# Four heads' scores in one run over four PSUM banks, with the transpositions in the dense products' banks

## What is computed

```python
qkv = x @ c_attn_w + c_attn_b                       # q, k, v
k = concat([img @ uk_w.T + uk_b, k_word], axis=1)   # one image key in front
v = concat([img @ uv_w.T + uv_b, v_word], axis=1)
scores = einsum('bhqd,bhkd->bhqk', q, k) / sqrt(32) # causal: kj <= qi + 1
attn = softmax(scores + mask)
x = x + (einsum('bhqk,bhkd->bhqd', attn, v) @ c_proj_w + c_proj_b)
xw = x @ Wx + b
h_t = tanh(h_{t-1} @ Wh + xw_t)                     # 512 steps, one after the other
return x + h
```

## Time and profile before

| | |
|---|---|
| median of 3 runs | 1696.64 us (1696.03 to 1708.65) |
| the profiled execution | 1703.19 us, its span 1701.4 us |
| mean granted TensorE clock | 0.981 |
| TensorE busy | 1613.0 us (95%), 32749 matmul instructions |
| VectorE busy | 792.6 us (47%) |
| ScalarE busy | 661.7 us (39%) |
| GpSimd busy | 185.6 us (11%) |
| moved by DMA | 130.24 MB, mean 77 GB/s |

### The profile page before, as it was taken

One profiled execution on the slowest core, in us unless ns is written; L12 is line 12 of the kernel. 1 busy time (PEld: TensorE's weight loads), 2 busy tenths in 40 slices (PEclk: granted clock), 3 DMA queues, 4 the chain that ended last, 5 costly groups with the idle time before them and its releaser, 6 DMA issues.

```text
span 1701.4 us, 74131 instructions
## 1 busy us (share of the span) xinstructions
PE 1613.0 (95%) x32749; PEld 1254.3 (74%) x32749; DVE 792.6 (47%) x2687; ACT 661.7 (39%) x2257; POOL 185.6 (11%) x300
## 2 busy tenths in 40 slices
PE   7889999999999999999999999999999999999775
PEld 6667777777777878777777877777777777777554
DVE  3444444454445454454545555454554554554221
ACT  3434333433334443443444444444434444443111
POOL 2111111111011010111011010110101111000000
PEclk9869999999999999999999999999999999999999
DMA  6322111222223122332323323233332443321000
GB/s 232 87 50 70 42 54 52 69 65 61 56 59 92 57 83 67 85 83 69 83 62 110 103 83 90 65 115 97 91 86 72 124 111 99 93 71 34 15 9 15
DMA packets 167903, 130.24 MB, mean 77 GB/s; under 512 B 54264, under 2 KB 153112, under 8 KB 167072
## 3 DMA queue, kind: packets, MB, share of 16 engines
q1 hardware_dynamic: 153792, 92.92, 19.3%
q0 software_dynamic: 13792, 32.58, 6.8%
HBM read 100.00 MB, written 25.43 MB: 74 GB/s over the span
## 4 chain that ended last, share of the span: by engine, by line
PE 88%; issue 3%; ACT 3%; DVE 2%; DMA 2%; SPq 1%; POOL 0%; DVEq 0%; ACTq 0%; POOLq 0%
PE rec L1047 26%; PE turned L977 11%; PE scores L966 9%; PE dense L495 8%; PE dense L496 7%; PE dense L497 7%; PE rec L1038 6%; PE pv L994 5%; PE pv L1012 2%; PE scores L1047 2%; DVE pre L873 1%; ACT states L727 1%; PE dense L948 1%; PE dense L1054 1%; DMA xin<-x 1%
## 5 line engine op out<-in xcount | busy, mean ns | idle before, releaser
L1047 PE MATMUL rec<-wh,states 128*32 128x128 f32 x15360 | 516.9, 275 | 28.8 <-ACT states L727 27.4
L1047 PEld LDWEIGHTS rec<-wh,states 128*32 128x32 f32 x15360 | 400.1, 110 | 125.3 <-ACT states L727 67.9
L679 ACT ACTIVATE probs<-probs,nmax 128x64 f32<-128x64 f32 (+7 forms) x512 | 270.6, 529 | 250.0 <-DVE nmax L818 247.5
L873 DVE STREAM_TRANSPOSE pre<-rec 128x128 f32<-128x128 f32 x480 | 151.8, 316 | 450.6 <-PE rec L1047 449.0
L727 ACT ACTIVATE states<-pre 128x32 f32<-128x32 f32 x512 | 133.0, 260 | 450.8 <-DVE pre L873 448.9
L818 DVE CUSTOM_DVE_ANT_0 probs<-scores,msk,nimg 128x64 f32<-128x64 f32 (+7 forms) x512 | 245.6, 514 | 38.8 <-PE scores L966 31.6
L977 PE MATMUL turned<-ident,probs 128*128 128x128 f32 (+1 forms) x1280 | 242.4, 291 | 8.7 <-ACT probsT L686 8.0
L977 PEld LDWEIGHTS turned<-ident,probs 128*128 128x128 f32 (+1 forms) x1280 | 132.4, 135 | 82.9 <-issue 68.6
L966 PE MATMUL scores<-kt,q 32*64 32x64 f32 (+7 forms) x2048 | 186.1, 431 | 0.3 <-DVE nmax L818 0.2
L827 DVE COPY probsT<-turned 128x128 f32<-128x128 f32 (+3 forms) x256 | 124.9, 488 | 77.1 <-PE turned L977 71.7
L495 PE MATMUL dense<-xT_hi,wqkv_hi 128*128 128x256 f32 x488 | 150.9, 309 | 1.4 <-DVE xT_lo L775 1.4
(11 more groups left out here) (148 smaller groups left out, 1779.9 us busy)
## 6 DMA issues: line engine op xcount, KB each, us to landing
vbuf<-v_dram SPq DMA_DIRECT2D x64, 192.0 KB, 2.8
xin<-x SPq DMA_DIRECT2D x64, 128.0 KB, 3.0
v_dram<-vbuf POOLq DMA_DIRECT2D x64, 128.0 KB, 2.7
out<-outs POOLq DMA_DIRECT2D x32, 256.0 KB, 4.2
vbuf<-v_dram SPq DMA_DIRECT2D x64, 128.0 KB, 2.4
kt<-k_dram SPq DMA_DIRECT2D x16, 512.0 KB, 4.1
vbuf<-v_dram SPq DMA_DIRECT2D x32, 256.0 KB, 3.3
k_dram<-knew POOLq DMA_DIRECT2D x60, 128.0 KB, 2.6
```

What stands on the lines that cost most here:

```text
L679: act.activation(probs[:, g % PROBS, 0:n], probs[:, g % PROBS, 0:n], ACT.Exp, scale=-1.0, bias=nmax[:, e, h:h + 1], accum_out=rowsum[:, e, ...
L873: dve.transpose(pre_all, rec_bank(g // GROUP)[:, 0:P]).then_inc(pre_ready, 1)
L1047: last = pe.matmul(rec_bank(g // GROUP)[Q * j:Q * j + Q, 0:P], state_tile(g - 1)[:, f, :], wh[:, f, P * j:P * j + P], start=False, stop=f ...
```

## The change

- The banks: `scores` has four banks, `turned` is gone, and the transpositions become jobs of the dense banks, in the same turn as the dense products. The semaphores `turned_copied` go with it; a copy of a transposition signals `dense_copied` of its bank.
- The scores of four units are issued together, at every fourth slot, in place of two at every second. The scores of unit g wait for the minimum of unit g − 4. No recurrence step is laid inside a run.
- The minimum and the exponential become an event of their own (`softmax`): its place in the four slots of a run is written by:

```diff
-            if u % 2 == 0:
-                emit([("score", v, 0, 0.07 + 0.107 * keys(g) / P) for v in (u, u + 1)])
+            if u % HC == 0:
+                emit([("score", v, 0, 0.06 + 0.06 * keys(g) / P) for v in range(u, u + HC)])
+            emit([("softmax", v, 0, 0.0) for v in ((u,), (u, u + 1), (u + 1,), ())[u % HC]])
...
             share -= side[0][3]
             emit([side.pop(0)])
+            if out[-1][0] == "vfirst":
+                share -= side[0][3]
+                emit([side.pop(0)])
...
-                if main[at][0] == "score" and main[at][1] % 2 == 0:
+                if main[at][0] == "score" and main[at][1] % HC < HC - 1:
                     continue
...
-        if kind in DENSE_KINDS and kind != "v":
+        if kind in DENSE_KINDS + ("turn",) and kind != "v":
             count = 2 if ("xsteps", 0, 0) in JOB else 3
...
-        scores = [ctx.enter_context(nc.psum_tensor(f"scores{i}", [P, BANK], F32)) for i in range(2)]
-        turned = [ctx.enter_context(nc.psum_tensor(f"turned{i}", [P, BANK], F32)) for i in range(2)]
+        scores = [ctx.enter_context(nc.psum_tensor(f"scores{i}", [P, BANK], F32)) for i in range(HC)]
...
+        def turns_copied(group):
+            return dict((JOB["turn", g, 0][0], JOB["turn", g, 0][1] + 1) for g in range(HC * group, HC * group + HC))
...
                 elif kind == "turn" and g % 2:
-                    act.copy(probsT[:, g % TURNED, 0:n], turned[1][:, 0:n]).then_inc(turned_copied[1], 1)
+                    act.copy(probsT[rows, g % TURNED, 0:n], bank(kind, g, 0)[rows, 0:n]).then_inc(copied(kind, g, 0), 1)
...
                 elif kind == "turn" and g % 2 == 0:
-                    dve.tensor_copy(probsT[:, g % TURNED, 0:n], turned[0][:, 0:n]).then_inc(turned_copied[0], 1)
+                    dve.tensor_copy(probsT[rows, g % TURNED, 0:n], bank(kind, g, 0)[rows, 0:n]).then_inc(copied(kind, g, 0), 1)
...
-                    if g > 1:
-                        pe.wait_ge(shifted_ready, g - 1)
+                    if g == 0:
+                        pe.wait_ge(image_ready, 1)
+                    if g >= HC:
+                        pe.wait_ge(shifted_ready, g - HC + 1)
...
-                        last = pe.matmul(scores[g % 2][W * b:W * b + W, 0:n], q[rows, trip % 2, c, at:at + W],
+                        last = pe.matmul(scores[g % HC][W * b:W * b + W, 0:n], q[rows, trip % 2, c, at:at + W],
                                          heads_tile(group)[rows, b, :], start=True, stop=True, skip_group_check=True)
...
                 elif kind == "turn":
-                    if g > 1:
-                        pe.wait_ge(turned_copied[g % 2], g // 2)
+                    wait_bank(pe, kind, g, 0)
...
                 elif kind == "pv":
-                    for parity in range(2):
-                        pe.wait_ge(turned_copied[parity], 2 * g + 2)
+                    for held, count in turns_copied(g).items():
+                        pe.wait_ge(dense_copied[held], count)
```

More of the change, by code:

```diff
@@ L60 @@
 LAGS = {
-    "DVE": {"xsplit": 0.7, "k": 0.2, "v": 0.2, "imgscore": 0.2, "score": 0.2, "turn": 0.2, "imgprob": 0.0,
+    "DVE": {"xsplit": 0.7, "k": 0.2, "v": 0.2, "imgscore": 0.2, "softmax": 0.2, "turn": 0.2, "imgprob": 0.0,
             "total": 0.5, "norm": 0.2, "attnlow": 0.9, "proj": 0.2, "step": 0.1, "hist": 0.8,
             "vimg": 0.2, "wproj": 0.8},
-    "ACT": {"xsplit": 0.0, "q": 0.2, "score": 0.8, "turn": 0.2, "imgprob": 0.2, "imgturn": 0.2,
+    "ACT": {"xsplit": 0.0, "q": 0.2, "softmax": 0.8, "turn": 0.2, "imgprob": 0.2, "imgturn": 0.2,
             "rowturn": 0.2, "norm": 0.6, "step": 0.5, "out": 0.2, "wproj": 0.0},
@@ L417, in attention_recurrence @@
         turned_ready = sem("turned_ready")
-        turned_copied = [sem(f"turned_copied{i}") for i in range(2)]
         pv_done = sem("pv_done")
@@ L652, in _ @@
                 high_qkv(i)
-            for f, d in enumerate(scores + turned):
+            for f, d in enumerate(scores):
                 act.wait_ge(setup_turned, C + 2 + f)
@@ L673, in _ @@
                                    bias=bqk[:, 0, i:i + 1]).then_inc(copied(kind, g, i), 1)
-                elif kind == "score":
+                elif kind == "softmax":
                     trip, u = divmod(g, UNITS)
@@ L682, in _ @@
                     n = P * tiles_of(g // UNITS)
+                    rows = slice(0, min(P, keys(g // UNITS)))
                     act.wait_ge(turned_ready, g + 1)
@@ L778, in _ @@
                     dve.wait_ge(setup_product, 2)
[L779 removed]
+                    dve.tensor_tensor(vimg_all, scores[0][:, :], uvb, ALU.add).then_inc(image_ready, 1)
                     dve.wait_ge(image_ready, 1)
@@ L817, in _ @@
                         wait_copied(dve, "imgscore", trip, h // HC)
-                    dve.tensor_tensor_reduce(out=probs[:, g % PROBS, 0:n], in0=scores[g % 2][:, 0:n],
+                    dve.tensor_tensor_reduce(out=probs[:, g % PROBS, 0:n], in0=scores[g % HC][:, 0:n],
                                              in1=msk[:, e, 0:n], scale=-SCALE, scalar=nimg[:, trip % 2, e, h:h + 1],
@@ L936, in _ @@
                     for f in range(C):
-                        last = pe.matmul(turned[0][:, :], rbc[:, f, :], wh[:, f, :], start=f == 0, stop=f == C - 1)
+                        last = pe.matmul(scores[0][:, :], rbc[:, f, :], wh[:, f, :], start=f == 0, stop=f == C - 1)
                     last.then_inc(setup_product, 1)
@@ L971, in _ @@
                     pe.wait_ge(probs_ready, g + 1)
-                    if g == 0:
-                        pe.wait_ge(image_ready, 1)
-                    if g > 1:
-                        pe.wait_ge(turned_copied[g % 2], g // 2)
+                    wait_bank(pe, kind, g, 0)
                     for at in range(0, n, P):
-                        last = pe.transpose(turned[g % 2][0:min(P, n - at), at:at + P],
+                        last = pe.transpose(bank(kind, g, 0)[0:min(P, n - at), at:at + P],
                                             probs[:, g % PROBS, at:min(at + P, n)], ident[:])
```

1 line of the change is left out of this document (removed).

## The result

| | before | after |
|---|---|---|
| median | 1701.71 us (6 runs) | 1689.34 us (6 runs, 1683.58 to 1695.25) |
| ratio, 95% interval | 1 | 0.9927 [0.9898, 0.9955] |
| span of the profiled execution | 1701.4 us | 1688.7 us |
| TensorE busy | 1613.0 us | 1538.8 us |
| span less TensorE busy | 88.4 us | 149.9 us |

The account below looks back on a forecast made before the run. TensorE, busy 95% of the span, was taken as the bound. The terms −79 + 34 + 6 = −39 us took the profiled 1703.2 us to 1664, carried to the median 1658 us, 2.3% faster, range 1622 to 1700.

Parts of the forecast that it names:

- The run (−79): Attention scores on TensorE: four heads in one run cost about a pair's time, 86 us in place of 165.
- Rival D: Score line: the four-bank run costs two pairs, saves nothing, bank waits stay; 1735 us, slower, chance 0.10.
- the estimate from the Trainium skill: Score runs: four heads take 1.30 pairs, so the saving would be 58 us and not 79.
- The shared banks (+34): Transpositions in the dense products' banks: TensorE waits for late copies cost 34 us, ends +10 and +57.
- The count from the timeline, 53 us: Shared banks: walking 893 jobs with two banks in turn found 103 late copies, together 53 us.
- The two reductions: Shared banks, cuts for spreading the maxima: −11 for the two dearest kinds of late copy, −6 for small cases.
- A little help to the small cases, −6: Shared banks: VectorE's and ScalarE's work spread more evenly takes 6 us off the small late copies.
- about 4 because the jobs come closer: Shared banks: removed score work brings TensorE's jobs closer together, adding about 4 us of waits.
- The recurrence (+6): Recurrence steps waiting for their tanh: shorter gaps give back 6 us of the saving, at most 12.
- The moves with one answer (0): Maxima, probabilities' buffer, first copies, key tiles and their loads, image values, GpSimd's queue: each put at 0 us.
- A: The forecast case: run price halved, 30 to 50 us given back; 1645 to 1675 us, chance 0.58.
- C: Gain given back entirely: runs 0.17 us dearer than pairs, all bank waits stand; 1695 us, 1675 to 1713, chance 0.15.

Follow-up runs that it names:

- b_shared: Kernel before, score pairs kept, transpositions moved into the dense products' two banks: 1753.04 us, 1.030 of before.
- c_img: c_x with VectorE's copy of the image scores put ahead of the totals, reciprocal and spread: 1659.40 us, 0.975 of before.
- b_three: b_shared with a third bank in the turn for dense work and transpositions: 1706.76 us, 1.002 of before.
- c_x: Changed kernel with the x tile loaded in two halves and its split placed 1.0 us later: 1667.45 us, 0.980 of before.
- b_halves: Kernel before with the x tile loaded in two halves, each after its own two projections: 1691.46 us, 0.994 of before.
- b_remedies: Kernel before with x loaded in halves, its split 1.0 us later and the image scores' copy ahead of the totals: 1702.41 us, 1.000 of before.
- a_late: Changed kernel with the x tile's split placed 1.5 us later in ScalarE's and VectorE's lists: 1673.74 us, 0.984 of before.
- c_first: c_img with the score run issued ahead of its slot's transposition: 1684.29 us, 0.989 of before.
- a_even: Changed kernel with one maximum and one exponential in each of a run's four slots: 1715.13 us, 1.008 of before.
- c_early: c_img with a run's second maximum and exponential placed in the first slot with the first: 1663.33 us, 0.977 of before.

## Why the forecast was right in sign and wrong in size

**The run (−79): right.** The lines of the timeline that answer to the earlier trace rows, for 64 keys and for 512:

```profile
74.68 0.37 PE L978 MATMUL scores<-kt,q 32*64 32x64 f32 x16
74.98 0.39 PE L502 MATMUL dense<-xT_hi,wqkv_hi 128*128 128x256 f32 x1
...
1480.71 1.11 PE L978 MATMUL scores<-kt,q 32*64 32x512 f32 x16
1481.76 1.08 PE L1047 MATMUL rec<-wx,x 128*32 128x128 f32 x32
```

0.30 us and 1.05 for four heads, where a pair cost 0.28 and 1.02: the eight added instructions cost 0.03, as taken. Added up over all scores of the two traces, from each start to the next start less the waits, it is 169.2 us before and 90.5 after, −78.7. By form, against the earlier trace rows, busy us fell while one instruction takes the same 613 ns, so twice as many run at a time:

```profile
L978 PE MATMUL scores<-kt,q 32*64 32x512 f32 x256 | 18.0, 613 | 0.0
...
L978 PE MATMUL scores<-kt,q 32*64 32x64 f32 x256 | 7.2, 259 | 0.4 <-DVE nmax L826 0.4
```

Rival D is out. So is the estimate from the Trainium skill (TensorE: Matmul & The Clock Gate, Part 3, the measured speedups), by which four row tiles would have taken 1.30 of our pairs: here they took 1.03 with 512 keys, the count nearest to the page's case.

**The shared banks (+34): mis-sized, and this is the first failed step.** The count from the timeline, 53 us, was good: b_shared measured 51. (The kernel's own list has 896 such jobs, three more than the 893 that I walked.) The two reductions were not equally good. The spread order did remove the row transposition's wait: in the changed kernel that copy ran at 1344.76, ahead of the exponential at 1345.57 and not behind one as in the earlier trace rows, and L1014 waits 0.2 us for it in all. But the wait behind the image scores' copy stayed, 6.6 us, since VectorE's totals, reciprocal and spread still stood ahead of it, which c_img cured (the prediction had named them itself, beside the two maxima); the projections stayed, 4.2 us, as the earlier trace rows said. "A little help to the small cases, −6" had no row behind it. And "about 4 because the jobs come closer" looks too small: transpositions wait 10.2 us for VectorE's copy of an earlier transposition alone, which before stood at 0.5. Together the bank waits are 39 us, 30 more than before; at b_shared's rate (36 us of idle time for 51 of time) my estimate of their cost is 42 us in place of the 34. The page TensorEngine Tiling (Array Packing) of the Trainium skill says in PSUM Bottleneck that after a tiling speedup the copies out of PSUM may become the limit. The trace agrees in part: bank waits went from 9.6 to 39.3 us of 1688.7, with TensorE still busy 91%; b_three, in the order of before, shows that it is how soon a bank is used again, not the copies' throughput.

**The recurrence (+6): right, once the x tile is out.** In c_x the tanh waits are 31.2 (+4). The waits for the bias of the recurrence's inputs, 9.6 (+5.5), were not in the forecast; with them it is +9, inside the bound of 12. In the changed kernel itself the tanh shows +14, of which 10.6 went with the x wait (41.8 to 31.2).

**The moves with one answer (0): the second failed step, and the dearest.** I wrote that the loads are issued where they were and that no DMA is moved past another. Both are true, SyncE's list is the same in both kernels, and were not the question. The x tile's load begins after a copy that TensorE's pace sets and took some 4 us in both traces at the place shown; what covers it is the TensorE work between. The change takes score work out of just those slots, and with it the split moved ahead of a step's tanh in ScalarE's list. At this kernel's ScalarE the wait had been 18.7 us already, visible in the list of waits of before, which I hadn't read for ScalarE since ScalarE was only 39% busy. c_x puts its price at 22 us in time, but by b_halves and b_remedies not all of it need be the change's: the early load brought 10 us in the kernel before too, and with the late split nothing. What is the change's own lies between the 5 us of the medians with the early load alone and the 22. The transpositions' waits for an exponential, which the forecast doesn't have, are mostly the same thing: 0 before, 7.7 in the changed kernel, 2.4 in c_x. The maxima ahead of a score run (0.4 us), the probabilities' buffers, key tiles, image values and GpSimd were 0 as said.

**The sum.** −79 + 34 + 6 = −39 was forecast, −12.4 measured. With the terms as measured or estimated above it is −79 + 42 + 9 = −28, and the x tile's 5 to 22 us bring it to between −23 and −6. The other way round, with c_x's 22 taken back it is −34, and with the image copy's 8 also −42. That c_img comes out near the forecast 2.3% is luck: it mends one thing that the forecast had not seen and one that it had priced. The measured 1689 us lies outside A's range (1645 to 1675) and in C's (1675 to 1713), for a part of C's reason (most bank waits stood) and for one that no rival named; C's dearer run did not come.

**Open.** How much of a_late's gain is the tanh's place ahead of the split and how much the shorter wait was not taken apart, nor was what b_halves gained. The price of neighbouring transpositions was not measured by itself: c_first took away the triples, not the neighbours, and no kernel spaced them evenly. Nor was the four-bank run tried with a third bank for the rest, for which there is no bank left. The bias waits (+5.5) were not followed further.

## What to carry to other kernels

When work is taken off the bound engine, list every load whose start hangs on that engine's progress and whose user stands in an in-order list, and compare its length with the work left between: idle time on an engine that is 40% busy is free only until a short, urgent instruction stands behind it. Where lists are sorted by planned clocks, compare the lists too: changed weights reorder instructions that nobody meant to move. Count a shared buffer's late copies from the trace job by job, as was done here, and don't discount the count for an order that does not move those very copies. And keep a packed run whole: one late member can cost a second run's time, and the list of waits shows a small part of it.

## What the runs showed of the hardware

**A wait inside a run of packed matmuls costs the concurrency on top of the wait.** In a_even 39 split runs were 28.5 us longer than unsplit ones, while the waits for the maximum in TensorE's list are 8.1 us, in 8 places, and belong for one half to a single one:

```profile
PE scores L978 <- DVE nmax L826: 8.1, 8, 3.8
```

**The clock fell in the middle of the work.** Right at the x tile's wait, behind 4.00 us of which TensorE was busy for 1.23, the changed kernel's granted clock went to half, 1.2 in place of 2.4 GHz (windows with TensorE's busy us, clock, DMA share, GB/s):

```profile
949.20:953.20 4.00, 1.23 (x9) 1.00 0.67 163
953.30:956.50 3.20, 2.92 (x48) 0.50 0.67 202
957.00:960.00 3.00, 3.00 (x49) 1.00 0.02 5
```

The step that started there took 1.93 us in place of 1.08. Between 240 us and the end of the attention the changed kernel has four such stretches of 3.4 us, and a fifth near 1554; the kernel before has one of 6.8, near 1564. At this place the wait of 2.73 us so cost 0.85 more than itself. They don't come from the x tile's wait alone: c_x, without it, has three of 3.4 us and one of 6.8 after 240 us.

**The granted clock differs from run to run and from kernel to kernel.** Runs of the kernel before beside c_x and c_img took from 1692.2 us at a mean granted clock of 0.989 to 1710.7 at 0.975. The means of each kernel's runs go from 0.974 (a_even) to 0.988 (c_early), against 0.980 for the kernel before. How much of that is the kernel's own doing is not shown, so a difference of a few microseconds between two kernels should be read beside their clocks.
